# Exponential in two pieces, first attention's scores from high and low parts, maxima ahead of the scaling of the context

## The reference

```python
h = jnp.concatenate([tok(x), txt], axis=1)
h = h + attn0(layernorm(h))   # one head of 64, scores not scaled
h = h + ffn0(layernorm(h))    # mean over tokens picks two experts
h = h + attn1(layernorm(h))   # two heads of 32
h = h + ffn1(layernorm(h))
h = h + attn2(layernorm(h))   # cosine similarity, top 64 of 1536, softmax
h = h + ffn2(layernorm(h))
h = h + attn3(layernorm(h))   # four heads of 16, relative positions
h = h + ffn3(layernorm(h))    # causal attention in groups, then experts

def attn(x):                  # 0, 1 and 3, a head
    p = softmax(q @ k.T, axis=-1)
    return p @ v
```

## Time and profile before

| | us |
|---|---|
| median of three runs | 5632.31 |
| lowest, highest | 5630.87, 5649.04 |
| profiled execution | 5644.55 |
| its span, first to last instruction | 5642.7 |
| mean granted TensorE clock | 0.822 |

### The profile page before, as it was taken

How to read it: one execution, slowest core, us unless ns; L and a number is a source line. 1 busy time by engine, 2 the same in 40 slices (tenths; PEclk the granted TensorE clock), 3 DMA queues, 4 the chain that set the end, 5 groups by cost and what they waited for, 6 DMA issues and landing times.

```text
span 5642.7 us, 71238 instructions
## 1 busy us (share of the span) xinstructions
PE 4372.6 (77%) x26536; PEld 2924.2 (52%) x26536; DVE 3331.4 (59%) x9075; ACT 1815.6 (32%) x2723; POOL 425.7 (8%) x484
## 2 busy tenths in 40 slices
PE   6886755799888755699888755699887765699987
PEld 4554544555646534555546534555546544555646
DVE  4444769555545669555555669555555659655554
ACT  2232521144332522134332422134332421234432
POOL 0100000011100000011100000021100000011100
PEclk9898865699988975599988975699988975689988
DMA  2000000000000000000000000000000000000000
GB/s 80 3 3 15 1 16 1 1 1 1 1 1 4 1 16 1 1 1 1 1 1 4 1 16 1 1 1 1 1 1 4 1 1 1 1 1 1 1 1 4
DMA packets 28309, 26.48 MB, mean 5 GB/s; under 512 B 10550, under 2 KB 26934, under 8 KB 27450
## 3 DMA queue, kind: packets, MB, share of 16 engines
q1 hardware_dynamic: 27962, 21.98, 1.4%
HBM read 20.40 MB, written 1.57 MB: 4 GB/s over the span
## 4 chain that ended last, share of the span: by engine, by line
PE 49%; DVE 29%; issue 5%; POOL 4%; ACT 3%; DVEq 1%; SPq 0%; POOLq 0%; ACTq 0%
PE ps L581 10%; PE ps L615 7%; DVE qup L759 4%; PE ps L1584 3%; DVE x L757 3%; PE ps L1600 3%; DVE x L761 3%; DVE ctxt L802 3%; PE ps L642 3%; DVE ctxt L798 2%; POOL st L394 2%; PE ps L915 2%; PE ps L414 2%; PE ps L427 2%; DVE row_max L1047 2%
## 5 line engine op out<-in xcount | busy, mean ns | idle before, releaser
L615 PE MATMUL ps<-cst,big 128*128 128x128 f32 x4608 | 674.9, 298 | 345.0 <-ACT big L717 312.5
L615 PEld LDWEIGHTS ps<-cst,big 128*128 128x128 f32 x4608 | 570.1, 154 | 426.3 <-ACT big L717 354.9
L698 ACT COPY big<-ps 128x512 f32<-128x512 f32 x816 | 478.6, 586 | 877.1 <-PE ps L615 877.1
L832 DVE TENSOR_REDUCE negmax<-ps 128x1 f32<-128x1536 f32 x336 | 590.1, 1757 | 64.0 <-PE ps L588 44.8
L717 ACT ACTIVATE big<-ps,negmax 128x1536 f32<-128x1536 f32 x336 | 518.7, 1544 | 269.0 <-DVE negmax L832 269.0
L409 PE MATMUL ps<-cst 128*128 128x512 f32 x608 | 332.5, 707 | 127.4 <-DVEq L187 58.2
L394 POOL TENSOR_TENSOR st<-st,cst 128x6 f32<-128x6 f32 x104 | 156.8, 1508 | 3449.3 <-DVE st L382 3445.2
L581 PE MATMUL ps<-kup,qup 128*128 128x512 f32 (+3 forms) x768 | 358.1, 563 | 41.8 <-POOLq L187 41.0
L588 PE MATMUL ps<-qlo 128*128 128x512 f32 x576 | 343.9, 736 | 7.4 <-DVEq L187 7.4
L422 ACT COPY xt<-ps 64x512 f32<-64x512 f32 x144 | 80.7, 579 | 828.0 <-PE ps L414 828.0
L642 PE MATMUL ps<-big,v 128*32 128x128 f32 (+1 forms) x8064 | 324.7, 278 | 8.1 <-DVE ctxt L1071 6.0
(11 more groups left out here) (317 smaller groups left out, 7131.4 us busy)
## 6 DMA issues: line engine op xcount, KB each, us to landing
rw<-in_w_route SPq DMA_DIRECT2D x128, 64.5 KB, 1.8
cst<-in_consts SPq DMA_DIRECT2D x1, 2671.0 KB, 14.7
cst<-in_consts SPq DMA_DIRECT2D x1, 2670.5 KB, 8.8
big<-in_consts SPq DMA_DIRECT2D x1, 1872.5 KB, 22.0
out_dram<-res SPq DMA_DIRECT2D x4, 384.0 KB, 2.8
experts_in<-in_consts SPq DMA_DIRECT2D x1, 1360.0 KB, 17.5
qup<-in_patches SPq DMA_DIRECT2D x4, 260.0 KB
klo<-in_pe_low SPq DMA_DIRECT2D x2, 384.0 KB, 23.3
```

The source lines that it names most:

```text
L615: ins = nc.tensor.transpose(turned_bank(kind, u, g)[:, i * P:(i + 1) * P], prob[:, slot_of(kind, u), (4 * g + i) * P:(4 * g + i + 1) * P], ...
L698: copy(pt[:, slot_of(kind, u), g, 0:n], turned_bank(kind, u, g)[:, 0:n]).then_inc(*ph.mark(copier(kind, g)))
L832: nc.vector.tensor_reduce(negmax[:, u:u + 1], flat[:, 0:n], AX.X, ALU.max, negate=True)\
```

## The change

Five edits.

1. `exps` in attentions 0, 1 and 3 becomes two instructions, columns 0 to 1023 and 1024 to 1535, each with its own accumulated sum (`part_sum`) and its own signal. The transposes of groups 0 and 1 wait for the first piece, those of group 2 for the second. POOL adds the two sums (`sum_rows`), and `give` waits for that (`rows_summed`).
2. Attention 0's scores take float32r operands: q as high part on partitions 0 to 63 and low part on 64 to 127 of `q_stack`, k in two tiles, its high part on both halves and its low part on both halves. Each bank of scores is two accumulated matmuls (high k, then low k) in place of one fp32 matmul.
3. The phase embed makes these: DVE first writes the weights of q and k twice side by side (`twice`), PE's six matmuls have 128 output partitions, ACT writes the high parts, DVE the difference. POOL's clearing of the upper half goes.
4. On PE, join(u-1) goes behind all three banks of scores(u+2).
5. On DVE, give(u-1) goes behind maxima(u+2).

```diff
+        part_sum = sb("part_sum", [P, 48, 2])
+        twice = big[:, 0:2 * P].rearrange("p (w r d) -> p w r d", w=2, r=2)
...
-        def qkv_pe(ph, pe, wq, wk, wv):
+        def qkv_blocks():
+
+            return [(w, j) for j in range(NB) for w in range(2)]
+
+        def qkv_pe(ph, pe):
             keep_clock(1, 9)
             pe.wait_ge(*ph.after("normed", 1))
             transpose_pe(ph, x, [0, 1, 2])
-            for j in range(NB):
+            pe.wait_ge(*ph.after("weights_spread", 2))
+            for i, (w, j) in enumerate(qkv_blocks()):
                 pe.wait_ge(*ph.after("xt_copied", j + 1))
-                nc.tensor.matmul(ps[0:D, 3 + j, :], W(wq), xt[:, 512 * j:512 * (j + 1)], start=True, stop=True)\
-                    .then_inc(*ph.mark("q_psum"))
-            for j in range(NB):
-                nc.tensor.matmul(ps[0:D, (6 + j) % 8, :], W(wk), xt[:, 512 * j:512 * (j + 1)], start=True, stop=True)\
-                    .then_inc(*ph.mark("k_psum"))
-            rows_pe(ph, W(wv), xt, [1, 2], "v_psum")
+                nc.tensor.matmul(ps[:, (3 + i) % 8, :], twice[:, w, :, :].rearrange("p r d -> p (r d)"), xt[:, 512 * j:512 * (j + 1)], start=True, stop=True)\
+                    .then_inc(*ph.mark("stack_psum"))
+            rows_pe(ph, W("v0"), xt, [1, 2], "v_psum")
 
         def qkv_act(ph, act):
             transpose_act(ph, act, xt, [0, 1, 2])
-            for j in range(NB):
-                act.wait_ge(*ph.after("k_psum", j + 1))
-                nc.scalar.copy(kt[0:D, 512 * j:512 * (j + 1)], ps[0:D, (6 + j) % 8, :])
-
-        def qkv_vec(ph, dve, scale):
-            for j in range(NB):
-                dve.wait_ge(*ph.after("q_psum", j + 1))
-                nc.vector.tensor_scalar(qt[0:D, 512 * j:512 * (j + 1)], ps[0:D, 3 + j, :], scale, None, ALU.mult)
+            for i, (w, j) in enumerate(qkv_blocks()):
+                act.wait_ge(*ph.after("stack_psum", i + 1))
+                nc.scalar.activation((q_stack, k_stack)[w][:, 0, 512 * j:512 * (j + 1)].bitcast(F32R), ps[:, (3 + i) % 8, :],
+                                     ACT.Identity).then_inc(*ph.mark("high_ready"))
+
+        def qkv_vec(ph, dve):
+            for i, (w, j) in enumerate(qkv_blocks()):
+                cols = slice(512 * j, 512 * (j + 1))
+                dve.wait_ge(*ph.after("high_ready", i + 1))
+                if w == 0:
+                    ins = nc.vector.scalar_tensor_tensor(q_stack[D:P, 0, cols].bitcast(F32R), ps[D:P, (3 + i) % 8, :], 1.0,
+                                                         q_stack[D:P, 0, cols], ALU.mult, ALU.subtract)
+                else:
+                    ins = nc.vector.scalar_tensor_tensor(k_stack[:, 1, cols].bitcast(F32R), ps[:, (3 + i) % 8, :], 1.0,
+                                                         k_stack[:, 0, cols], ALU.mult, ALU.subtract)
+                ins.then_inc(*ph.mark("low_ready"))
...
         def attn_pool(ph, pool, kind):
-            link = pool_chain(ph, pool)
+
             for u, (hd, q) in enumerate(units_of(kind)):
...
+                if kind.startswith("attn3"):
+                    if u >= 2:
+                        pool.wait_ge(*ph.after("side_ready", u - 1))
+                    nc.gpsimd.tensor_copy(qz[64:80, u % 2, :], qlo[64:80, hd % 2, q * P:(q + 1) * P])\
+                        .then_inc(*ph.mark("queries_alone"))
+                    pool.wait_ge(*ph.own("queries_alone"))
+                if u >= 1:
+                    sum_rows(ph, pool, u - 1)
+            sum_rows(ph, pool, len(units_of(kind)) - 1)
+
+        def sum_rows(ph, pool, u):
+
+            pool.wait_ge(*ph.after("probs_ready", 2 * (u + 1)))
+            nc.gpsimd.tensor_tensor(rowsum[:, u:u + 1], part_sum[:, u, 0:1], part_sum[:, u, 1:2], ALU.add)\
+                .then_inc(*ph.mark("rows_summed"))
+            pool.wait_ge(*ph.own("rows_summed"))
...
+                elif kind == "attn0":
+                    for part in range(2):
+                        ins = nc.tensor.matmul(bank, q_stack[:, 0, qs].bitcast(F32R), k_stack[:, part, lo * P:hi * P].bitcast(F32R),
+                                               start=(part == 0), stop=(part == 1))
...
-                if g == 0:
+                if kind == "attn2" and g == 0:
                     pe.wait_ge(*ph.after("probs_ready", u + 1))
+                elif kind != "attn2" and g != 1:
+                    pe.wait_ge(*ph.after("probs_ready", 2 * u + 1 + g // 2))
...
                 if u > 0:
                     context(u - 1)
-                for j in range(2 if ahead else 0):
+                for j in range(NB if ahead else 0):
                     scores(u + 2, j)
                 if u > 0:
                     join(u - 1)
-                if ahead:
-                    scores(u + 2, 2)
                 if ahead and kind.startswith("attn3"):
                     side(u + 2)
...
+                for k, cols in enumerate((slice(0, 1024), slice(1024, S))):
+                    nc.scalar.activation(prob[:, slot_of(kind, u), cols], src[:, cols], ACT.Exp, bias=bias,
+                                         accum_out=part_sum[:, u, k:k + 1]).then_inc(*ph.mark("probs_ready"))
...
-                dve.wait_ge(*ph.after("probs_ready", u + 1))
+                dve.wait_ge(*(ph.after("probs_ready", u + 1) if kind == "attn2" else ph.after("rows_summed", u + 1)))
...
                 copy_group(ph, dve, kind, u, 1, nc.vector.tensor_copy)
                 if u > 0:
                     take(u - 1)
-                    give(u - 1)
                 if u + 2 < len(units):
                     if kind.startswith("attn3"):
                         place_side(u + 2)
                     maxima(u + 2)
+                if u > 0:
+                    give(u - 1)
...
-                clear_upper(ph, pool)
                 norm_pool(ph, pool, 1)
...
+                for w, name in enumerate(("q0", "k0")):
+                    nc.vector.tensor_copy(twice[:, w, :, :], W(name).unsqueeze(1).to_broadcast([P, 2, D]))\
+                        .then_inc(*ph.mark("weights_spread"))
```

More of the change, by code:

```diff
@@ L51 @@
 SIGNALS = {
-    "embed": {"pool_step": 1, "rstd_ready": 2, "xt_copied": 3, "emb_psum": 1, "xt_psum": 3, "q_psum": 3, "k_psum": 3,
+    "embed": {"weights_spread": 2, "rstd_ready": 2, "xt_copied": 3, "emb_psum": 1, "xt_psum": 3, "stack_psum": 6, "high_ready": 6, "low_ready": 6,
         "v_psum": 2, "vec_step": 13, "var_ready": 2, "normed": 1},
-    "attn0": {"strips_ready": 12, "strips_copied": 12, "probs_ready": 12, "pt_by_act": 24, "scores_ready": 12, "pt_psum": 36, "ctx_ready": 12,
+    "attn0": {"strips_ready": 12, "strips_copied": 12, "probs_ready": 24, "rows_summed": 12, "pt_by_act": 24, "scores_ready": 12, "pt_psum": 36, "ctx_ready": 12,
         "max_ready": 12, "pt_by_vec": 12, "vec_step": 12, "ctx_copied": 12},
@@ L552, in attn_pool @@
         def attn_pool(ph, pool, kind):
-            link = pool_chain(ph, pool)
             for u, (hd, q) in enumerate(units_of(kind)):
-                if u >= 2:
-                    pool.wait_ge(*ph.after("side_ready", u - 1))
-                nc.gpsimd.tensor_copy(qz[64:80, u % 2, :], qlo[64:80, hd % 2, q * P:(q + 1) * P]).then_inc(*ph.mark("queries_alone"))
-                pool.wait_ge(*ph.own("queries_alone"))
+                if kind.startswith("attn3"):
[12 more added lines that the diff above has]
+            pool.wait_ge(*ph.own("rows_summed"))
         def attn_pe(ph, pe, kind):
@@ L716, in exps @@
                     act.wait_ge(*ph.after("pt_psum", before_groups(kind, u - 1)))
-                nc.scalar.activation(prob[:, slot_of(kind, u), 0:n], src, ACT.Exp, bias=bias,
-                                     accum_out=rowsum[:, u:u + 1]).then_inc(*ph.mark("probs_ready"))
+                if kind == "attn2":
+                    nc.scalar.activation(prob[:, slot_of(kind, u), 0:n], src, ACT.Exp, bias=bias,
+                                         accum_out=rowsum[:, u:u + 1]).then_inc(*ph.mark("probs_ready"))
+                    return
+                for k, cols in enumerate((slice(0, 1024), slice(1024, S))):
+                    nc.scalar.activation(prob[:, slot_of(kind, u), cols], src[:, cols], ACT.Exp, bias=bias,
+                                         accum_out=part_sum[:, u, k:k + 1]).then_inc(*ph.mark("probs_ready"))
             def copy_row(u):
@@ L1151, in _ @@
                 pool.wait_ge(consts_in, CONST_DMAS)
-                clear_upper(ph, pool)
                 norm_pool(ph, pool, 1)
                 ph.leave(pool)
-                Phase(led, "attn0").leave(pool)
+                ph = Phase(led, "attn0")
+                attn_pool(ph, pool, "attn0")
+                ph.leave(pool)
                 ph = Phase(led, "mean0")
@@ L1170, in _ @@
                 ph.leave(pool)
-                Phase(led, "attn1").leave(pool)
+                ph = Phase(led, "attn1")
+                attn_pool(ph, pool, "attn1")
+                ph.leave(pool)
```

(4 more changed lines are left out.)

6 lines of the change are left out of this document (3 added, 3 removed).

## The result

The changed kernel takes 5829.2 us (median of four runs, 5814.0 to 5836.4); the kernel before, run beside it on the same chip, 5631.6 (5630.0 to 5649.0). The ratio is 1.0333, 95% interval 1.0302 to 1.0364 (the quotient of the two medians, 1.0351, lies inside it). The medians differ by 198 us. The profiled execution took 5826.27 us (before 5644.55), its span is 5824.4 us, and the mean granted clock rose from 0.822 to 0.844. The prediction was 5838.

What follows compares the result with a forecast made beforehand. The prediction took PE to bound attentions 3 and 0, and the exp-transposes-copies chain attention 1. Its +212, +19 and -25 made +206: 5644.55 profiled became 5850, 12 lower for the median, so 5838 us, range 5795 to 5885.

Steps and rivals of the forecast that it cites:

- What waits for `give`: Attentions 0, 1, 3: context(u-1) waits for give(u-2), now behind maxima(u+1), whose scores PE issues behind context(u-2).
- The turn of attention 3: Attention 3, from one context to the next: 7.21 us against 5.84, +1.37, 21 times in each of 8 stages.
- side until DVE: Attention 3: PE's side matmuls until DVE starts behind them, 0.71 us of the 7.21.
- Ends and heads of attention 3: Attention 3, each stage: 2.0 us less at the end and 0.3 less in the first unit.
- the sum: Whole kernel: attention 3 +212, attention 1 +19, attention 0 -25, together +206 us.
- Attention 1, predicted +19: Attention 1: a unit of 4.04 us against 3.74, +0.30, 21 times in 4 stages, less 1.6 a stage.
- Attention 0, predicted -25: Attention 0: a unit of 5.40 us against 5.77, -0.37, 9 times in 4 stages; -1.25 and -1.6 a stage.
- The edits costed at nothing: Exp pieces in steady units, POOL's sums, scores order in attentions 1 and 3, stage ahead of attention 0: each nothing.
- the ring: Attentions 0, 1, 3: context, scores, (join, side), maxima, give, next context wait in a circle without slack; chance 0.87.
- The clock: Rival: the clock falls in attentions 1 and 3, +214 us, so 6052 us; chance 0.06.
- the 1.3 to 1.6 foretold: Attention 3: PE's first context load waits 1.3 to 1.6 us for DVE's L1071 operation in every unit.
- the eight terms of the ring: Attention 3's 7.21 us: context, scores, join, side matmuls, masked copies, maximum, reciprocal, scaling with wait.

Runs made afterwards that it cites:

- run 3: The changed kernel with the joined context in PSUM bank 7 and the wait for `ctx_copied` moved from context(u) to join(u): 5577.0 us, ratio 0.9907.
- run 9: The kernel before with two more memsets of 64x1536 and a drain on DVE in the set-up, no stage changed: 5625.3 us, ratio 0.9979.
- Run 5: The kernel before with only the exp in two pieces and the sums on POOL added: 5564.6 us, ratio 0.9866.
- run 10: The changed kernel run once more without any change, for a second profile: 5831.5 us.

## Why the prediction was right, step by step

**What waits for `give`.** Right. The step from the earlier trace rows and the code, that `context(u-1)` waits for a `give` which now stands behind maxima that need work behind that context, is what the profile after shows in every steady unit, and run 3 shows that both halves of it are needed.

**The turn of attention 3, predicted 7.21, measured 7.32.** By terms, measured from the timeline above: context 0.79 (0.79), scores 2.69 (2.67), join 0.14 (0.14), side until DVE 0.79 (0.71), masked copies 0.67 (0.66), maximum 1.67 (1.67), reciprocal 0.19 (0.19), scaling and wait 0.38 (0.38). Nearly all of the miss is one term, and its size stood in the rows: the bank behind the join took 0.94 from its start to that of the side matmuls (1268.84 to 1269.78), where I charged two records at 0.43. What follows the join costs 0.08 more, be it a bank or, as now, the side matmul (0.47 for 0.38). Over 168 turns 0.11 is 18 us. The stages also begin with a turn of 7.60, which was not foreseen (+2).

**Ends and heads of attention 3, predicted -2.0 and -0.3 a stage.** Right in kind, the end 0.5 short in size. The drain as it came out (timeline, last ringed context and the one after it):

```profile
1525.47 0.86 PE L672 MATMUL ps<-big,v 128*32 128x128 f32 x24 [1.70 <-DVE ctxt L1105]
...
1528.42 0.85 PE L672 MATMUL ps<-big,v 128*32 128x128 f32 x22
```

That gap is 2.95 where the kernel before has 5.76, and the last one 2.16 for 2.47: -3.1 in the second halves. But the kernel before ran its ends at a lower clock. Its twelve transposes between the two contexts, and the same twelve in a stage of run 9 that kept the clock (timelines):

```profile
1493.01 2.82 PE L615 MATMUL ps<-cst,big 128*128 128x128 f32 x12 [0.47 <-ACT big L717]
```

```profile
1315.36 1.53 PE L615 MATMUL ps<-cst,big 128*128 128x128 f32 x12 [0.47 <-ACT big L717]
```

There the two gaps are 4.46 and 2.16. In the changed kernel the second halves kept the clock, the first halves didn't (4.3 and 2.4). So at equal clock the end is 1.5 shorter in both, and the other 1.6 in the second halves is the clock's. The mean of -3.1 and -1.5 lies near the forecast by luck. The heads are 0.3 shorter in the mean, from 1.3 less to 0.3 more. In all, attention 3 gave +236.6 for the predicted +212: its turns +257 for +230 (some 20 by their length, 2 by the first turns, 5 by the clock, below), its ends -19 for -16, its heads -2 as in the sum.

**Attention 1, predicted +19, measured +20.7.** The turn was 4.05 for 4.04; the gap at the end 0.8 shorter instead of the 1.3 in the sum (+2), the heads 0.7 shorter instead of 0.3 (-2).

**Attention 0, predicted -25, measured -18.6.** The turn was 5.45 for 5.40: from the first of the six float32r matmuls to the maximum it is 1.71 (215.76 to 217.47) where I had 1.65. That is 1.8 of the 6.4 over 36 turns. The gap at the end of the stage was only 0.14 shorter (3.60 for 3.74) instead of the 1.3 in the sum, which I had carried over from attention 1's rows to attention 0: some 4.6 over four stages. The heads gave 0.6 back.

**The edits costed at nothing.** Embed -1.0, right. POOL's sums 195 ns each, far under the 4 us that would matter. Exp in two pieces: within the ring nothing, as said, since exp starts ahead of the context. But that holds in the ring alone. Run 5 shows what it is worth with the ring open, 54 us in the attentions, some 13 of them the clock's, a good part of the others in attention 1's steady units (0.34 a unit), where the chain exp, transposes, copies sets the pace. The ring ate this gain; the prediction named the gain's cover without giving the price.

**The clock.** I put 0.06 on its fall in attentions 1 and 3. The stages kept 0.96 to 0.98 and 0.95 to 0.97, with a wait of 1.70 us in attention 3 for the 1.3 to 1.6 foretold, but not without a trace. In some stages one turn of 21 fell to a lower clock, as here between turns that did not (windows, attention 3 of pass 1):

```profile
2615.11:2622.52 7.41, 5.61 (x49) 3.77 (x50) 3.54 (x8) 3.04 (x7) 0.48 (x2) 1.00 0.00 1
2622.52:2631.53 9.01, 7.31 (x50) 4.71 (x51) 3.54 (x8) 3.04 (x7) 0.48 (x2) 0.81 0.01 2
2631.53:2638.85 7.32, 5.62 (x50) 4.15 (x51) 3.54 (x8) 3.05 (x7) 0.48 (x2) 1.00 0.00 0
```

The same work takes 7.31 us of PE for 5.62. Three turns of 168 did this in the profile after and one in that of run 10, 1.7 us each, some 5 us in all. The Trainium skill (TensorE: Matmul & The Clock Gate, "What's actually happening") says that the throttled clock is the default and that activity releases it. These few turns may be a trace of that; over the stages, with PE busy 77%, the clock of attention 3 did not fall against the kernel before (0.97).

**What was not in the prediction** is the rest, -56 us in the profiled execution (-40 in run 10), through a higher clock in stages whose code is the same. It hid an undershoot: in the touched stages the profiles differ by 238 us where the sum had 206. Against the medians' 198 the 238 leaves some 40 for it, an estimate, since the kernel before was profiled in a long execution and the changed one was not. The 5838 against 5829 is thus closer than the working deserves. The mechanism and seven of the eight terms of the ring hold; the total owes part of its fit to two misses of opposite sign.

## What to carry to other kernels

When an instruction is moved behind another on its engine, list who waits for its semaphore and what the new predecessor itself waits for; if the two lists meet, the order closes a ring and each turn costs the sum of its parts, however busy the engines looked. A buffer of its own (here a spare PSUM bank) lets the wait go to the one instruction that needs it. Measure edits one at a time: four of these five won 90 us in the attentions together (114 between the medians, the clock's share included), and the fifth hid that. An engine's one stall can also be cured by asking last for what comes last (banks 0, 2, 1: 0.29 us a unit).

## What the runs showed of the hardware

- Stages with the same instructions took 54.8 or 50.85 us, and 121.6 or 118.0 us, in profiles of two programs, at granted clocks of 0.78 or 0.85 and 0.86 or 0.91. Summed over a profile this moved up to 56 us (1%), more than the 48 us that the float32r scores won in attention 0; executions of one program differ by up to 54 us with their mean clock (run 3). A comparison by stage leaves most of this out, not all: attention 3 of the changed kernel took 1490.9 and 1483.5 us.
- The ends of attention 3 fell to the lower clock in all eight stages of one profile of the kernel before, and in six and seven of eight in two others; twelve transposes then took 2.5 to 2.8 us for 1.53.
- What followed a matmul of 16 columns cost 0.08 us more than in a row of 512-column matmuls, a 512-column bank (1268.84 before) as well as a side matmul (1219.34 after).
- Exp of 1536 columns in two pieces takes ACT 1.11 and 0.68 us, with an accumulator read of 0.19 to 0.20 behind each; from the first start to the end of the last read that is 1.88 us (1215.27 to 1217.15). One piece took 1.54 and its read as long as one of these, with an overlap of 0.1, 1.63 in all. The split costs ACT 0.25 us a unit, where I had taken 0.4.
- A PE that is busy 77%, with a gap of 1.7 us in every 7.3, kept a granted clock of 0.96 to 0.98 over eight stages.
